# FFN norm variance over the features, Newton step on GpSimd, masks written into the score banks by ScalarE, and another slot order

## The reference

```python
def attn_layer(x, Wqkv, qs, ksc, Wo):
    q, k, v = ...                      # x @ Wqkv, 16 heads of 64
    q = l2norm(q) * qs                 # q / |q|: one reciprocal root per token and head
    k = l2norm(k) * ksc
    q = q * cos * scale + rotate_half(q) * sin * scale
    k = k * cos * inv + rotate_half(k) * sin * inv
    out = local_attention(q, k, v)     # 32 queries see their window and the one before; masked softmax
    return out @ Wo

def ffn_layer(x, g, bln, W1, b1, W2, b2):
    mu = x.mean(-1, keepdims=True)
    var = ((x - mu) ** 2).mean(-1, keepdims=True)
    xn = (x - mu) / jnp.sqrt(var + 1e-05) * g + bln
    a, gate = jnp.split(xn @ W1 + b1, 2, -1)
    return a * jax.nn.gelu(gate, approximate=False) @ W2 + b2
```

## Time and profile before

| | us |
|---|---|
| median of 3 runs | 3552.26 |
| the profiled execution | 3551.83 |
| its span, first to last instruction | 3550.0 |
| PE busy | 3451.3 (97%) |
| DVE busy | 3216.1 (91%) |
| ACT busy | 2734.4 (77%) |
| POOL busy | 2583.4 (73%) |

### The profile page before, as it was taken

How to read it: one execution, slowest core, us unless ns; L and a number is a source line. 1 busy time by engine, 2 the same in 40 slices (tenths; PEclk the granted TensorE clock), 3 DMA queues, 4 the chain that set the end, 5 groups by cost and what they waited for, 6 DMA issues and landing times.

```text
span 3550.0 us, 112382 instructions
## 1 busy us (share of the span) xinstructions
PE 3451.3 (97%) x44743; PEld 2622.1 (74%) x45216; DVE 3216.1 (91%) x5485; ACT 2734.4 (77%) x4727; POOL 2583.4 (73%) x2267
## 2 busy tenths in 40 slices
PE   8998899999999999999999999999999999999998
PEld 6775577777777777777777777777777777777776
DVE  6876999999999999999999999999999999999995
ACT  5665687787887788788788778778878878877876
POOL 3334878777778777777877877877877877777772
PEclk9999999999999999999999999999999999999999
DMA  1001212212212212211221221221221221122121
GB/s 47 24 2 46 49 42 57 57 44 55 54 37 57 66 38 52 54 48 46 66 50 39 54 57 38 66 51 40 53 57 44 60 51 47 39 75 51 35 51 41
DMA packets 61717, 171.67 MB, mean 48 GB/s; under 512 B 9488, under 2 KB 21264, under 8 KB 60816
## 3 DMA queue, kind: packets, MB, share of 16 engines
q1 hardware_dynamic: 61200, 164.46, 18.1%
HBM read 21.82 MB, written 4.19 MB: 7 GB/s over the span
## 4 chain that ended last, share of the span: by engine, by line
PE 95%; issue 2%; ACT 1%; DVE 1%; POOL 1%; DVEq 0%; POOLq 0%; ACTq 0%
PE bank L1017 11%; PE bank L998 10%; PE bank L959 10%; PE bank L1033 9%; PE bank L911 9%; PE bank L1366 8%; PE bank L982 7%; PE bank L912 7%; PE bank L910 5%; PE bank L1379 4%; PE bank L976 3%; PE bank L379 2%; PE bank L359 2%; PE bank L344 2%; PE bank L1334 1%
## 5 line engine op out<-in xcount | busy, mean ns | idle before, releaser
L1273 POOL TENSOR_TENSOR rotbuf<-mbuf 128x512 f32<-128x512 f32 x768 | 969.3, 1273 | 511.2 <-PE bank L959 322.6
L1287 POOL TENSOR_TENSOR rotbuf<-rotbuf,rs 128x512 f32<-128x512 f32 x768 | 786.7, 1045 | 66.2 <-DVE rs L1203 66.2
L1137 DVE TENSOR_REDUCE ss<-sq 128x8 f32<-128x512 f32 x768 | 516.1, 677 | 156.5 <-ACT sq L1059 156.4
L1297 POOL TENSOR_TENSOR probs<-probs,rden 128x768 f32<-128x768 f32 x384 | 564.5, 1470 | 121.4 <-DVE rden L1239 121.4
L1156 DVE TENSOR_TENSOR mbuf<-bank,table 128x512 f32<-128x512 f32 x768 | 527.9, 687 | 13.4
L1157 DVE TENSOR_TENSOR mbuf<-bank,table 128x512 f32<-128x512 f32 x768 | 522.1, 680 | 0.0
L1059 ACT ACTIVATE sq<-bank 128x512 f32<-128x512 f32 x768 | 457.8, 596 | 55.5 <-PE bank L912 22.6
L1017 PEld LDWEIGHTS bank<-probs_t,vbuf 96*64 96x64 f32 x12288 | 390.2, 138 | 144.4 <-issue 104.3
L1079 ACT ACTIVATE kbuf<-bank 128x512 f32<-128x512 f32 x384 | 217.4, 591 | 347.7 <-PE bank L959 347.7
L911 PE MATMUL bank<-weights,inputs 128*128 128x512 bf16 x1152 | 439.5, 382 | 36.8 <-issue 14.4
L959 PE MATMUL bank<-ident,rotbuf 128*128 128x128 f32 x3072 | 451.7, 275 | 13.8 <-DVE mbuf L1157 7.6
(11 more groups left out here) (112 smaller groups left out, 6056.7 us busy)
## 6 DMA issues: line engine op xcount, KB each, us to landing
vbuf<-v_stage SPq DMA_DIRECT2D x192, 384.0 KB, 4.4
vbuf<-v_stage SPq DMA_DIRECT2D x192, 256.0 KB, 4.0
vbuf<-v_stage SPq DMA_DIRECT2D x96, 128.0 KB, 4.5
stage<-in_wqkv SPq DMA_DIRECT2D x36, 256.0 KB, 5.1
weights<-in_wo SPq DMA_DIRECT2D x6, 512.0 KB, 6.6
out_t<-weights SPq DMA_DIRECT2D x1, 2048.0 KB, 6.3
weights<-out_t SPq DMA_DIRECT2D x1, 2048.0 KB, 9.8
out_t<-weights SPq DMA_DIRECT2D x16, 128.0 KB, 2.3
```

The lines of the kernel that those rows point to most:

```text
L1137: e.tensor_reduce(b.ss[:, col:col + 8], b.sq[:, u % 2, :].rearrange("p (h d) -> p h d", h=8), AX_X, ALU.add).then_inc(s.sq_summed, 1)
L1273: e.tensor_tensor(b.rot[:, u, :], b.m1[:, u % 2, :], b.m2[:, u % 2, :], ALU.add).then_inc(s.rotated, 1)
L1287: e.tensor_tensor(v, v, r, ALU.mult).then_inc(s.scaled, 1)
L1297: e.tensor_tensor(probs, probs, b.rden[:, p % 2, :].unsqueeze(2).broadcast_to([P, 8, BLOCK_K]), ALU.mult).then_inc(s.probs, 1)
```

## The change

1. **Variance.** One matmul with the 1/128 matrix gives the variance of each token on all 128 feature rows at once ([128, 256]). The detour through `ss` and `pe_ff_rstd` with its ring place `rb` are gone. ACT takes log, exponential (with log 1/2 in the bias) and a square of 2w on [128, 256]; DVE does a Newton step with two `scalar_tensor_tensor` on [128, 256] and multiplies with a third.
2. **Newton step of q/k.** It moves from DVE (3 instructions on 66 columns) to POOL (4 on 64 columns).
3. **Masks.** The four mask matmuls per unit of scores are gone. `act_mask`, one ACT copy of 128x768 (bf16 mask in, f32 out), writes the pair of score banks, and the score matmuls wait for it (`masked`).
4. **Order.** The ring has 26 places in place of 27. As 26 is no multiple of 3 the bank now rotates from slot to slot, so `work_bank` takes the instance. All four slot lists are written anew; the FFN pieces stand nearer to the attention of their instance.

```diff
@@ pe_scores_of
-    e.wait_ge(s.shifted, k.c[4] + p)
+    e.wait_ge(s.masked, k.c[4] + (p + 1))
...
-    for blk_half, parity in ((0, 0), (1, 1), (0, 1), (1, 0)):
-        ...
-        e.matmul(b.scores[parity][c, 0:4 * BLOCK_K].rearrange("p (h k) -> p h k", h=4), b.identb[r, r], mask,
-                 start=True, stop=False, skip_group_check=True)
@@
+def act_mask(e, s, b, at, ahead, p):
+    ...
+    e.wait_ge(s.shifted, k.c[4] + p)
+    mask = b.maskb[:, 2 + p // 2, :].unsqueeze(1).unsqueeze(1).broadcast_to([P, 2, 4, BLOCK_K])
+    e.activation(b.score_pair.rearrange("p b (h k) -> p b h k", h=4), mask, ACT.Copy).then_inc(s.masked, 1)
@@ pe_ff_variance
-    for t in range(2):
-        mm = e.matmul(work_bank(b, "mu", 0)[:, N_TOK + t:N_TOK + t + 1], b.ff_sq[:, P * t:P * (t + 1)], b.inv_dim[:, 0:1], ...)
+    e.matmul(work_bank(b, k, "mu", 0)[:, N_TOK:2 * N_TOK], b.inv_dim[:, :], b.ff_sq[:, :], start=True, stop=True)
-def pe_ff_rstd(e, s, b, at, ahead):
-    ...
@@
+def act_ff_seed(e, s, b, at, ahead):
+    ...
+    w = b.ff_w[:, :]
+    e.activation(w, work_bank(b, k, "mu", 0)[:, N_TOK:2 * N_TOK], ACT.Ln, bias=b.ff_consts[:, 0:1])
+    e.activation(w, w, ACT.Exp, bias=b.ff_consts[:, 1:2], scale=-0.5)
+    e.activation(b.ff_sq[:, :], w, ACT.Square, scale=2.0)
+def dve_ff_refine(e, s, b, at, ahead):
+    ...
+    e.scalar_tensor_tensor(a, work_bank(b, k, "mu", 0)[:, N_TOK:2 * N_TOK], LN_EPS, a, ALU.add, ALU.mult)
+    e.scalar_tensor_tensor(w, a, 3.0, w, ALU.subtract, ALU.mult)
@@ dve_ff_norm
-    e.tensor_tensor(b.ff_xc[:, k.par, :], b.ff_xc[:, k.par, :], work_bank(b, "rb", 0)[:, 0:N_TOK], ALU.mult)
+    e.scalar_tensor_tensor(x, x, -1.0, b.ff_w[:, :], ALU.mult, ALU.mult)
-def dve_refine(e, s, b, at, ahead):
+def pool_refine(e, s, b, at, ahead):
     e.tensor_tensor(a, y, y, ALU.mult)
-    e.scalar_tensor_tensor(a, a, -0.5, x, ALU.mult, ALU.mult)
-    e.scalar_tensor_tensor(y, a, 1.5, y, ALU.add, ALU.mult)
+    e.tensor_tensor(a, a, x, ALU.mult)
+    e.tensor_scalar(a, a, -0.5, 1.5, ALU.mult, ALU.add)
+    e.tensor_tensor(y, y, a, ALU.mult)
```

More of the change, by code:

```diff
@@ L192, in __init__ @@
         self.ok = 0 <= m < SEQS
-        self.c = {per: per * (FIRST_N + m) for per in (1, 2, REFINE_OPS, PAIRS)}
+        self.c = {per: per * (FIRST_N + m) for per in (1, 2, FIRST_REFINE, PAIRS)}
         self.cols = slice(m * N_TOK, (m + 1) * N_TOK)
@@ L1090, in act_copy_v @@
         e.wait_ge(s.v_placed[t], k.c[PLACED[t]])
-    e.activation(b.vstage[:, t, 512 * half:512 * (half + 1)], work_bank(b, "v", i)[:, :], ACT.Copy).then_inc(s.v_copied, 1)
+    e.activation(b.vstage[:, t, 512 * half:512 * (half + 1)], work_bank(b, k, "v", i)[:, :], ACT.Copy).then_inc(s.v_copied, 1)
+def act_mask(e, s, b, at, ahead, p):
+    k = at(ahead)
+    if not k.ok:
+        return
+    e.wait_ge(s.shifted, k.c[4] + p)
+    if k.m == 0 and p == 0:
+        e.wait_ge(s.x_ready, s.first_done)
+    mask = b.maskb[:, 2 + p // 2, :].unsqueeze(1).unsqueeze(1).broadcast_to([P, 2, 4, BLOCK_K])
+    e.activation(b.score_pair.rearrange("p b (h k) -> p b h k", h=4), mask, ACT.Copy).then_inc(s.masked, 1)
 def act_exp_of(e, s, b, at, ahead, p):
@@ L1175, in act_seed @@
 def act_seed(e, s, b, at, ahead):
-    k, ff = at(ahead), at(ahead - NORM_LAG)
-    if not (k.ok or ff.ok):
+    k = at(ahead)
+    if not k.ok:
         return
@@ L1425, in act_ff_gelu @@
     e.wait_ge(s.ff_gated, k.c[NF] + (c - 1))
-    e.activation(b.ff_ge[0:size, (k.m + c) % 2, :], work_bank(b, "up", c)[0:size, 0:N_TOK], ACT.Gelu,
+    e.activation(b.ff_ge[0:size, (k.m + c) % 2, :], work_bank(b, k, "up", c)[0:size, 0:N_TOK], ACT.Gelu,
                  bias=b.vecs[0:size, k.layer, 5 + c:6 + c]).then_inc(s.ff_gelu, 1)
@@ new lines, in pe_deep_slot @@
+    pe_ff_up(e, s, b, at, -2, 2)
+    pe_values_of(e, s, b, at, 0, 1)
+    pe_scores_of(e, s, b, at, 1, 0)
+    pe_transpose(e, s, b, at, 1, 6)
+    pe_values_in(e, s, b, at, 2, 0)
+    pe_project_in(e, s, b, at, 2, 7)
+    pe_ff_mean(e, s, b, at, -1)
+def act_deep_slot(e, s, b, at):
+    act_mask(e, s, b, at, -1, 0)
+    act_ff_gelu(e, s, b, at, -4, 2)
+    act_exp_of(e, s, b, at, -2, 3)
+    act_copy_t(e, s, b, at, -1, 6)
+    act_copy_out(e, s, b, at, -2, 1)
+    act_square(e, s, b, at, 0, 7)
+    act_copy_v(e, s, b, at, 0, 0)
+    act_ff_square(e, s, b, at, -3)
+    act_copy_pt_of(e, s, b, at, -2, 2)
+    act_ff_seed(e, s, b, at, -3)
+    act_seed(e, s, b, at, 0)
+    act_square(e, s, b, at, 1, 0)
+    act_mask(e, s, b, at, -1, 1)
+    act_copy_out(e, s, b, at, -2, 2)
@@ new lines, in dve_deep_slot @@
+    dve_sum_squares(e, s, b, at, 2, 4)
+    dve_rope(e, s, b, at, 2, 4)
+    dve_residual_of(e, s, b, at, -1)
+    dve_sum_squares(e, s, b, at, 2, 5)
+    dve_rope(e, s, b, at, 2, 5)
+    dve_max_of(e, s, b, at, 0, 3)
+    dve_ff_gate(e, s, b, at, -2, 0)
+    dve_shift(e, s, b, at, 0, 3)
+    dve_sum_of(e, s, b, at, 0, 2)
+    dve_ff_gate(e, s, b, at, -2, 1)
+    dve_sum_squares(e, s, b, at, 2, 6)
+    dve_rope(e, s, b, at, 2, 6)
+    dve_ff_gate(e, s, b, at, -2, 2)
+    dve_max_of(e, s, b, at, 1, 0)
@@ L1931, in constants @@
             masks[rows, 2 + t] = np.where(ok, 0.0, big)
-            masks[64 - 64 * half:128 - 64 * half, 4 + t] = masks[rows, 2 + t]
     half = np.arange(0, DIM_HEAD, 2, dtype=f)
```

328 lines of the change are left out of this document (151 added, 177 removed), and 8 rows, old and new, of the table WORK_RING.

## The result

The changed kernel takes 3490.77 us (median of four runs, 3488.58 to 3491.76), against 3554.41 us for the kernel before on the same chip: a ratio of 0.9822, 95% interval 0.9807 to 0.9838. That is 63.6 us less, where 77 were forecast. The profiled execution took 3491.41 us, its span is 3489.3 us, and the granted clock of PE is 0.993 over it (0.995 before).

The account below looks back on a forecast made before the run. PE was taken to set the 33.0 us slot. Saving 1.25 us (masks 0.76, spread 0.49) less 0.45 of stall gave 32.2; 0.8 times 96 is 77 us off 3551.8, so 3475 us, range 3422 to 3548.

Parts of the forecast that it names:

- the slot of 32.2 us: Steady slot: 31.75 us of PE work plus 0.45 of stall, against 33.0 before; chance 0.43.
- Masks, 0.76 a slot: On PE, dropping four mask groups at 0.19 us each saves 0.76 us a slot, at most 1.12.
- Spread, 0.49 a slot: On PE, the matmuls spreading the FFN norm's roots (L1349) go, saving all their 0.49 us a slot.
- Order, counted as nothing: New slot lists and 26 ring places: nothing else added, banks rotate at no cost.
- ACT at 31.23 us: ACT's busy time per slot rises from 26.43 to 31.23 us with mask copies and FFN seed, 98% of the slot.
- DVE at 30.24 us: DVE's busy time per slot falls from 30.79 to 30.24 us if nothing holds its new instructions.
- The lock: DVE instructions with two SBUF inputs wait for POOL, 0.92 us each if held alike; 0.45 counted, for the norm only.
- The stall of 0.45 at v 1: PE waits at the second product with v for pj 0's bank, part repeating at pj 1: 0.45 us a slot.
- Rival A: PE is never made to wait: slot 31.75 us, 120 us less, 3432 us; chance 0.21.
- B: Both new DVE instructions wait for POOL, DVE bounds the slot at 32.7 us: 3523 us; chance 0.21.
- C: ACT's strict-order queue becomes the bound, its waits partly surviving: slot 33.6 us, 3610 us; chance 0.11.
- Ramps unchanged: The ramps and the first block outside the steady slots stay as they are, at no change in time.

Follow-up runs that it names:

- seed_psum_maskpe: `seed_psum` with the deep layers' four mask matmuls put back on PE ahead of the scores: 3463.9 us, ratio 0.9748 to the kernel before.
- seed_psum: Changed kernel with ACT's q/k seed ahead of its FFN seed and the FFN refinement's first step written into PSUM: 3446.26 us, ratio 0.9701 to the kernel before.
- best: `seed_psum` with a final addition moved from DVE to POOL and the clamp back at 66 columns: 3440.91 us, ratio 0.9684 to the kernel before.
- before_masks_act: Kernel before with ACT writing the masks and no mask matmuls on PE; order, Newton step and variance as before: 4520.13 us, ratio 1.2728.
- relief: Changed kernel with the last layer's final addition moved from DVE to POOL and the clamp at 66 columns: 3485.32 us, ratio 0.981 to the kernel before.

## Why the prediction was right, and where not

The forecast of 3475 us was 16 us low, and the slot of 32.2 us is met (32.1). The terms behind it are less good than the sum.

- *Masks, 0.76 a slot.* Mis-sized. By the chain it is 0.13 us a unit and 0.5 a slot, for the scores behind take 0.82 us in place of 0.66. In the slot 0.32 (before's order) and 0.25 (new order, no loop) arrive. In the changed kernel as it stands, 2 us of the whole.
- *Spread, 0.49 a slot.* Right on the chain (a second one adds 0.44), and 0.37 arrive in the slot.
- *Order, counted as nothing.* This was the missing term. The slot of `seed_psum_maskpe`, with masks on PE, is 1.12 us shorter than before, and the spread explains 0.37 to 0.49 of it. The rest is 0.6 to 0.75. By the chain 0.39 of that are the up-projections, which cost less behind a transpose or a projection (0.2 go again into the transposes, as much and more comes from pauses that are gone), 0.11 the variance (taken as no change "within 0.1") and 0.08 the down-projection. No run changes the order alone.
- *ACT at 31.23 us.* It is 94% busy (304.81 us of 323.50), 30.3 us a slot, where 96% and more was forecast. The mask copy takes 807 ns (844 taken), and instructions that don't wait overlap by about 0.1 us, so busy time grows by less than their sum. The idle time before the copies of k, 217.3 us, is 7.7 us now, as forecast. These lines of 1000 to 2941 us answer to the earlier trace rows (the sum of squares, L1154, takes 681 ns, as before):

```profile
L1108 ACT ACTIVATE bank<-maskb 128x768 f32<-128x768 bf16 x241 | 194.4, 807 | 0.0
L1083 ACT ACTIVATE kbuf<-bank 128x512 f32<-128x512 f32 x241 | 144.1, 598 | 7.7 <-PE bank L969 0.5
...
L1474 DVE SCALAR_TENSOR_TENSOR ff_xc<-ff_xc,ff_w 128x256 f32<-128x256 f32 x61 | 36.0, 591 | 0.0
...
L1210 POOL TENSOR_TENSOR newton_a<-rs 128x64 f32<-128x64 f32 x60 | 29.7, 495 | 119.1 <-ACT rs L1199 119.1
...
L1186 DVE TENSOR_SCALAR newton_x<-ss 128x64 f32<-128x64 f32 x60 | 26.3, 439 | 2.1
L1463 DVE SCALAR_TENSOR_TENSOR ff_w<-ff_sq,ff_w 128x256 f32<-128x256 f32 x60 | 25.8, 430 | 2.1
```

- *DVE at 30.24 us.* It is 96% busy, 30.8 us a slot. The norm took 0.59 us (0.93 counted), the refinement 0.43 (0.48 counted). The clamp at 0.44, held by POOL, was not foreseen.
- *The lock.* For each new DVE instruction I asked only how long DVE would wait. That POOL would lose time to them I had written down ("Even with 1 us lost to DVE's two instructions 3.5 us are left") and dismissed by POOL's slack. That a wait of 0.2 us lies on the path I hadn't seen. Slack over a slot says nothing of a chain within it.
- *The stall of 0.45 at v 1.* The wrong place. PE waits for no bank at v 1: DVE's rope, which its waits were to name, ends one wait of a weight load in 60 slots (0.3 us). It waits for POOL's scaling at a transpose. I had seen that POOL's train starts 0.7 us later and hadn't followed it to its end. The size fits: taking the loop away shortens the slot from 32.1 to 31.6.
- *Rival A, 3432 us.* The floor of 31.75 is met (31.6 measured with `seed_psum`), though by the same cancelling of terms, and `best` comes within 9 us of that time. B is refuted: DVE stood at 32.7 only in the last layer, by the final addition. C's mechanism is real (`before_masks_act`) but not in the new order.
- *Ramps unchanged.* 8.8 us were lost ahead of the first residual. Within the stretch, the slots of the last layer cost 5.4 us more than ordinary ones, the five changes of layer 3.5, and the last three distances 2.4. That is why a slot 0.9 us shorter, more than the 0.8 forecast, gave 64 us and not 77. `relief` makes the last layer's slots ordinary, but its last three distances are 2.9 us longer, and its stretch is only 1.0 us shorter.

So the mask was over-counted by 0.5 us a slot and the order, with the variance, under-counted by 0.6 to 0.75. The sum was right by the cancelling of these errors, and the stall had the right size at the wrong place. That is luck, which a reader shouldn't take for accuracy.

## What to carry to other kernels

When four engines are above 85% busy in strict order, follow the chain of waits all the way round one slot, across engines, and price each edit by whether it lies on that round. Busy shares and slack per slot say nothing of it. When two instructions exclude each other, ask of both who comes second, also of the one whose row looks undisturbed. And test edits in pairs where the first can start what blocks it: the swap of the seeds alone gave nothing and the tensor in PSUM alone 19 us, the two together 45.

## What the runs showed of the hardware

- A DVE instruction with both inputs in SBUF and a POOL instruction hold each other up in both directions: behind POOL's train DVE's step takes 425 ns with one input in PSUM and 819 ns in the mean (1054 in the median) with two in SBUF, and POOL's small one takes 495 for 293 ns beside a DVE instruction that began 0.08 us earlier. The Trainium skill, page "SBUF — State Buffer", section "Summary: rules for kernel authors", says this of VectorE with two SBUF inputs, with whichever comes second waiting. The trace agrees on who waits; POOL's instruction still ends 0.15 us after DVE's (2019.16 against 2019.01), less than the 0.29 it takes alone. The cost to POOL is the half that I hadn't used.
- DVE's clamp of 128x64, a `tensor_scalar` that reads one tensor in SBUF, also waits for POOL: 0.50 us or 0.35, ending 0.05 us behind POOL's instruction in eight slots, against 0.18 in the kernel before.
- A group of 32 small score products takes 0.82 us on the chain when nothing of its kind stands ahead, and 0.66 behind four mask products that take 0.29 themselves. Taking the four off gave back 0.13 us of their 0.29.
- The four products of an up-projection take 1.06 us on the chain behind scores or a product with v, and 0.86 or 0.87 behind a transpose. Where a group stands in PE's list is part of its price: 0.39 us a slot here.
- ACT writes 128x768 values from bf16 in SBUF into PSUM in 807 ns, a little under the exponential of the same size (842 ns in the same stretch).
- A product's wait for its weights can hold PE up without standing in PE's own waits: a load that waited 0.45 us a slot made its eight products 0.17 us longer (1.04 for 0.87), in a stretch whose chain names PE alone.
